# Earlier LayerNorm batches and three-tile steps in the narrow groups of a graph-convolution kernel

## The reference

```python
def _layernorm(x, axis=-1, eps=1e-05):
    m = jnp.mean(x, axis=axis, keepdims=True)
    v = jnp.var(x, axis=axis, keepdims=True)
    return (x - m) / jnp.sqrt(v + eps)

    h = jnp.maximum(_layernorm(x, axis=-1), 0.0)
    support = jnp.matmul(h, W)
    out = jax.nn.relu(jnp.matmul(adj, support) + b)
    return x + out
```

## Time and profile before

| | before |
|---|---|
| median of 3 runs | 775.92 us (775.54 to 781.69) |
| the profiled execution | 775.09 us, of which span 773.3 us |
| mean granted TensorE clock | 0.979 |
| PE busy | 733.7 us (95%), 3120 products |
| DVE busy | 619.8 us (80%) |
| ACT busy | 526.0 us (68%) |
| POOL busy | 129.4 us (17%) |
| moved | 281.59 MB, 364 GB/s over the span |

### The profile page before, as it was taken

The page is one execution under the profiler, slowest core; times in us unless marked ns, Lnnn a source line. Parts: engine busy times, 40 slices in busy tenths (PEclk is TensorE's granted clock), DMA queues, the critical chain, the costliest instruction groups (busy, mean ns, idle before and its releaser), DMA issues.

```text
span 773.3 us, 7777 instructions
## 1 busy us (share of the span) xinstructions
PE 733.7 (95%) x3120; PEld 595.4 (77%) x3120; DVE 619.8 (80%) x297; ACT 526.0 (68%) x375; POOL 129.4 (17%) x86
## 2 busy tenths in 40 slices
PE   4899999999999999999999999999999999999997
PEld 3677777777777777888887888888888888888884
DVE  4778787878787877889877998888888888788885
ACT  5767676767676766676667777666666767677664
POOL 2444444444444444000000000000000000000000
PEclk9899999999999999999999999999999999999999
DMA  8999898999988887899999999999999999899993
GB/s 324 426 339 359 347 354 338 353 341 343 345 345 345 342 333 313 328 390 410 383 379 418 422 410 413 382 391 378 394 382 380 394 388 376 327 374 403 407 340 149
DMA packets 35604, 281.59 MB, mean 364 GB/s; under 512 B 4080, under 2 KB 4464, under 8 KB 11248
## 3 DMA queue, kind: packets, MB, share of 16 engines
q1 hardware_dynamic: 35568, 281.10, 92.9%
HBM read 276.89 MB, written 4.19 MB: 364 GB/s over the span
## 4 chain that ended last, share of the span: by engine, by line
PE 51%; issue 19%; POOL 16%; DMA 7%; DVE 3%; ACT 2%; SPq 1%; POOLq 0%; ACTq 0%; DVEq 0%
PE banks L444 50%; POOL z_sb L235 11%; DMA raw<-adj 7%; POOL rstd L227 5%; DVE low L416 3%; ACT high L308 2%; PE banks L462 0%; POOLq L72 0%; PE banks L464 0%; PE banks L463 0%; SPq L160 0%; SPq L179 0%; DVE sum_low L377 0%; ACT relu_out L279 0%; DVE x_sb L384 0%
## 5 line engine op out<-in xcount | busy, mean ns | idle before, releaser
L416 DVE TENSOR_TENSOR low<-raw,high 128x3072 fp32r<-128x3072 f32 (+1 forms) x190 | 570.1, 3004 | 110.0 <-PE banks L444 68.5
L308 ACT ACTIVATE high<-raw 128x3072 fp32r<-128x3072 f32 (+1 forms) x190 | 471.1, 2488 | 143.8 <-DMA raw<-adj 118.4
L444 PE MATMUL banks<-high,h_high 128*128 128x512 f32 x1024 | 272.0, 397 | 33.9 <-ACT h_high L256 22.8
L444 PE MATMUL banks<-high,h_low 128*128 128x512 f32 x1024 | 276.1, 402 | 0.0
L444 PE MATMUL banks<-low,h_high 128*128 128x512 f32 x1024 | 266.8, 393 | 1.2 <-DVE low L416 1.1
L444 PEld LDWEIGHTS banks<-high,h_high 128*128 128x128 f32 x1024 | 192.6, 189 | 82.2 <-issue 28.7
L444 PEld LDWEIGHTS banks<-high,h_low 128*128 128x128 f32 x1024 | 199.6, 195 | 42.9
L444 PEld LDWEIGHTS banks<-low,h_high 128*128 128x128 f32 x1024 | 194.6, 191 | 45.1 <-DVE low L416 3.9
L235 POOL TENSOR_SCALAR z_sb<-x_sb,neg_mean,rstd 128x128 f32<-128x128 f32 x64 | 90.6, 1426 | 1.8
L256 ACT ACTIVATE h_high<-z_sb 128x512 fp32r<-128x512 f32 (+2 forms) x17 | 10.3, 604 | 90.7 <-POOL z_sb L235 90.6
L227 POOL TENSOR_TENSOR rstd<-var_eps,minus_half 128x4 f32<-128x4 f32 (+2 forms) x17 | 38.4, 2260 | 166.5 <-DVE var_eps L353 166.5
(11 more groups left out here) (17 smaller groups left out, 28.7 us busy)
## 6 DMA issues: line engine op xcount, KB each, us to landing
raw<-adj SPq DMA_DIRECT2D x127, 1536.0 KB, 8.4
raw<-adj SPq DMA_DIRECT2D x63, 1024.0 KB, 6.5
x_sb<-x_blocks SPq DMA_DIRECT2D x16, 256.0 KB, 6.4
out_blocks<-x_sb SPq DMA_DIRECT2D x16, 256.0 KB, 7.6
x_sb<-x_rows SPq DMA_DIRECT2D x15, 256.0 KB, 9.0
raw<-adj SPq DMA_DIRECT2D x4, 512.0 KB, 6.9
raw<-adj SPq DMA_DIRECT2D x2, 256.0 KB, 3.4
x_sb<-x_rows SPq DMA_DIRECT2D x1, 192.0 KB, 3.3
```

What stands on the lines that cost most here:

```text
L308: nc.scalar.activation(high[:, t % HIGH_SLOTS, 0:columns(t)], raw[:, t % RAW_SLOTS, 0:columns(t)], ACT.Copy).then_inc(high_ready, 1)
L416: nc.vector.tensor_tensor(low[:, t % LOW_SLOTS, 0:columns(t)], raw[:, t % RAW_SLOTS, 0:columns(t)], high[:, t % HIGH_SLOTS, 0:columns(t)]. ...
L444: return nc.tensor.matmul(banks[:, FIRST_BANK[g] + c, :], h[:, (t - FIRST_STEP[g]) * DEPTHS[g] + k, :], tile[:, slot, at:at + BANK], start ...
```

## The change

Two things are changed together.

1. The LayerNorm batches are begun earlier. With j = t//4 + 3, mean of batch j is at t%4 = 0, the squares at t%4 = 1 and 2, the variance at t%4 = 2, and rectify and rectified_low of the batch before, j-1, at that same t%4 = 2. Batch m+3 has its mean at step 4m, its variance at 4m+2, its h at 4m+6, and PE takes it from step 4m+8 on. The loads of x are issued one batch earlier, the squares and the variance of batch 2 are moved ahead of step 1, and so are the mean of batch 3 and, on SP, the x of batches 3 and 4.
2. The narrow groups take three k-tiles a step: 21 steps of 3072 columns and a last one of one k-tile (depth_of), 22 in place of 32. The 2 x 22 narrow steps come at 3072 columns, as the wide ones do. Drains are at the steps 3, 6, 8, 11, 13, 16 of a group (in wide groups too), relu at +4, the store at +9. The host lays adj out accordingly.

```diff
@@ -13,10 +13,10 @@
 
 
 WIDTHS = [6, 2, 6, 2]
-DEPTHS = [1, 2, 1, 2]
+DEPTHS = [1, 3, 1, 3]
 FIRST_BLOCK = [0, 6, 8, 14]
 FIRST_BANK = [0, 6, 0, 6]
-STEPS = [TILES // d for d in DEPTHS]
+STEPS = [-(-TILES // d) for d in DEPTHS]
 FIRST_STEP = [sum(STEPS[:g]) for g in range(len(WIDTHS))]
 ALL_STEPS = sum(STEPS)
 LAST = ALL_STEPS - 1
@@ -33,8 +33,8 @@
 Z_SLOTS = 2
 
 
-DRAIN_AT, DRAIN_EVERY = 3, 4
-PROJECT_AFTER, RELU_AFTER, STORE_AFTER = 1, 5, 10
+DRAIN_AT = [3, 6, 8, 11, 13, 16]
+PROJECT_AFTER, RELU_AFTER, STORE_AFTER = 1, 4, 9
 OUT_SLOTS = 2
 EPS = 1e-5
 
@@ -49,6 +49,12 @@
     return max(g for g in range(len(WIDTHS)) if FIRST_STEP[g] <= t)
 
 
+def depth_of(t):
+
+    g = group_of(t)
+    return min(DEPTHS[g], TILES - (t - FIRST_STEP[g]) * DEPTHS[g])
+
+
 def x_slot(j):
 
     return max(j - 1, 0) % X_SLOTS
@@ -58,7 +64,7 @@
 
     for g in range(len(WIDTHS) - 1):
         for c in range(WIDTHS[g]):
-            if FIRST_STEP[g + 1] + DRAIN_AT + c * DRAIN_EVERY + after == t:
+            if FIRST_STEP[g + 1] + DRAIN_AT[c] + after == t:
                 return FIRST_BLOCK[g] + c
     return None
 
...
@@ -182,13 +185,15 @@
                     load_x(1)
                 if i == 1:
                     load_x(2)
+                if i == 2:
+                    load_x(3)
             sp.dma_start(W_sb[:, :], W).then_inc(params_landed, 16)
             sp.dma_start(bias[:, :], b).then_inc(params_landed, 16)
             for t in range(1, ALL_STEPS):
                 g = group_of(t)
                 s = t - FIRST_STEP[g]
-                if g == 0 and s % 4 == 1 and s // 4 + 3 < len(BATCHES):
-                    load_x(s // 4 + 3)
+                if g == 0 and s % 4 == 1 and s // 4 + 4 < len(BATCHES):
+                    load_x(s // 4 + 4)
                 if t >= RAW_SLOTS:
 
                     sp.wait_ge(low_ready, t - RAW_SLOTS + 1)
@@ -289,6 +294,7 @@
             opening(3)
             act.wait_ge(params_landed, 32)
             nc.scalar.activation(W_high[:, :], W_sb[:, :], ACT.Copy).then_inc(W_high_ready, 1)
+            square(2, range(4, 8))
             for t in range(1, ALL_STEPS):
                 g = group_of(t)
                 s = t - FIRST_STEP[g]
@@ -308,15 +314,16 @@
                     nc.scalar.activation(high[:, t % HIGH_SLOTS, 0:columns(t)],
                                          raw[:, t % RAW_SLOTS, 0:columns(t)],
                                          ACT.Copy).then_inc(high_ready, 1)
-                j = (t - 1) // 4 + 2
-                if g == 0 and j < len(BATCHES):
-                    first = BATCHES[j][0]
-                    if t % 4 == 1:
-                        square(j, range(first, first + 2))
+                if g == 0:
+
+                    j = t // 4 + 3
+                    if t % 4 == 1 and j < len(BATCHES):
+                        square(j, range(BATCHES[j][0], BATCHES[j][0] + 2))
                     if t % 4 == 2:
-                        square(j, range(first + 2, first + 4))
-                    if t % 4 == 0:
-                        rectify(j)
+                        if j < len(BATCHES):
+                            square(j, range(BATCHES[j][0] + 2, BATCHES[j][1]))
+                        if j - 1 < len(BATCHES):
+                            rectify(j - 1)
                 n = drained_at(t, 0)
                 if n is not None:
                     act.wait_ge(products_done, FIRST_STEP[group_of(t)])
@@ -391,10 +398,12 @@
             mean(1)
             opening(1)
             variance(1)
+            mean(2)
             opening(2)
             rectified_low(1)
             opening(3)
-            mean(2)
+            variance(2)
+            mean(3)
             dve.wait_ge(W_high_ready, 1)
             nc.vector.tensor_tensor(W_low[:, :], W_sb[:, :], W_high[:, :].bitcast(F32),
                                     ALU.subtract).then_inc(W_low_ready, 1)
@@ -417,14 +426,15 @@
                                             raw[:, t % RAW_SLOTS, 0:columns(t)],
                                             high[:, t % HIGH_SLOTS, 0:columns(t)].bitcast(F32),
                                             ALU.subtract).then_inc(low_ready, 1)
-                j = (t - 1) // 4 + 2
-                if g == 0 and j < len(BATCHES):
+                if g == 0:
+                    j = t // 4 + 3
+                    if t % 4 == 0 and j < len(BATCHES):
+                        mean(j)
                     if t % 4 == 2:
-                        variance(j)
-                    if t % 4 == 0:
-                        rectified_low(j)
-                        if j + 1 < len(BATCHES):
-                            mean(j + 1)
+                        if j < len(BATCHES):
+                            variance(j)
+                        if j - 1 < len(BATCHES):
+                            rectified_low(j - 1)
                 n = drained_at(t, 0)
                 if n is not None:
                     sum_to_low(n)
...
-        rows = adj[first * BANK:(first + width) * BANK].reshape(width, BANK, STEPS[g], depth, P)
-        arrays[f"adj{g}"] = np.ascontiguousarray(rows.transpose(2, 4, 0, 3, 1)) \
-            .reshape(STEPS[g], P, width * depth * BANK)
+        rows = adj[first * BANK:(first + width) * BANK].reshape(width, BANK, TILES, P)
+        for part, k0, k1, deep in (("", 0, TILES // depth * depth, depth), ("_end", TILES // depth * depth, TILES, 1)):
+            if k1 > k0:
+                tiles = rows[:, :, k0:k1].reshape(width, BANK, (k1 - k0) // deep, deep, P)
+                arrays[f"adj{g}{part}"] = np.ascontiguousarray(tiles.transpose(2, 4, 0, 3, 1)) \
+                    .reshape((k1 - k0) // deep, P, width * deep * BANK)
     ap = {name: nc.dram_tensor(name, a.shape, F32, kind="ExternalInput").ap() for name, a in arrays.items()}
     out = nc.dram_tensor("out_blocks", (COL_BLOCKS, P, BANK), F32, kind="ExternalOutput").ap()
-    gnn_layer(nc, ap["x_rows"], ap["x_blocks"], [ap[f"adj{g}"] for g in range(len(WIDTHS))],
-              ap["W"], ap["b"], out)
+    adj_groups = [[ap[f"adj{g}{part}"][s] for part in ("", "_end") if f"adj{g}{part}" in arrays
+                   for s in range(arrays[f"adj{g}{part}"].shape[0])] for g in range(len(WIDTHS))]
+    gnn_layer(nc, ap["x_rows"], ap["x_blocks"], adj_groups, ap["W"], ap["b"], out)
     result = run_bass_kernel_spmd(nc, [arrays], core_ids=[0]).results[0]["out_blocks"]
     return np.ascontiguousarray(result.transpose(0, 2, 1)).reshape(N, P)
```

## The result

| | before | after |
|---|---|---|
| median | 777.03 us (775.54 to 781.69, 4 runs) | 730.97 us (730.1 to 731.72, 4 runs) |
| the profiled execution | 775.09, span 773.3 | 730.47, span 728.7 |
| mean granted TensorE clock | 0.979 | 0.999 |
| PE / DVE / ACT / POOL busy | 95 / 80 / 68 / 17% | 98 / 85 / 72 / 18% |

The ratio of after to before is 0.9397, 95% interval 0.9354 to 0.9441: 6.0% faster. 731 was predicted, with 728 to 741 as the range.

A forecast was written before the change was run, and what follows sets the result against it. Group 0 was taken as bound by a chain over POOL, asked too late, and group 2 by PE. 773.3 - 37.7 - 3.0 - 3.6 = 729.0 us of span, plus 1.8, gave 731, range 728 to 741.

The forecast's parts named there:

- Group 0 from batch 2: 60 wide steps on PE without waits take 244.8 us in place of 282.56: -37.7 us.
- the clock: Lower TensorE clock in group 0 after PE stands still: 14.9 us lost, counted within the group 0 gain.
- one fall at the start: PE falls once to the lower clock level at the start, costing 1.7 to 3 us; allowed for in the range.
- POOL's cover: Group 0, variance to h: POOL takes 12 us, PE runs out only at about 17; cover 8 us a batch.
- rival 4: POOL in group 0 may wait out two DVE instructions: 20.9 us a batch, 30 us more, 798; chance 0.02.
- rival 2: Each POOL instruction in group 0 makes DVE's low wait its length: 21 us more, 752; chance 0.04.
- Transfers of group 0: A batch moves 6.55 MB, 15.3 us at 427 GB/s, under PE's 16.3, so PE is the limit.
- Rival 1: Transfers bound group 0 at 387 GB/s: 16.9 us a batch, 9 us more, 740; chance 0.10.
- The start: Before batch 2: PE starts step 1 at 18.5, batch 2 begins at 31.4 in place of 34.41: -3.0 us.
- Narrow groups: Three k-tiles a step remove small losses, 1.4 in group 1, 0.9 behind it, 1.3 at the end: -3.6 us.
- Drains: SP waits for a store in four places; costed at nothing, 2 us a place or 8 us without cover.
- Sum: Whole kernel: 773.3 - 37.7 - 3.0 - 3.6 = 729.0 us of span, 730.8 with 1.8 outside it; 731 predicted.

The follow-up runs named there:

- Both single experiments: Against the kernel before: only the earlier LayerNorm batches, 736.71 us, ratio 0.9505; only the deeper narrow steps with the new drain steps, 769.38 us, ratio 0.9929.

## Why the prediction was right, point by point

**Group 0 from batch 2: right.** 244.8 us were predicted for 60 steps, 244.80 measured. The sum was made from PE's side, old stretch less new, and it does not depend on how the old loss is split. The split was wrong: the prediction put 14.9 us down to the clock as a part of its own. The run with extra products shows that full speed brings at most 6.7 of it in group 0, since POOL's chain sets the period and the clock's loss lay mostly inside the wait. The 1.7 to 3 us that the range allowed for one fall at the start was given without a row. In the traces of four runs (only the deeper steps, h at its use, one and three more loads) many products of step 1 start 0.43 us apart, as at the lower clock: the step takes 5.8 to 6.3 us in place of 4.9, so 0.9 to 1.4.

**POOL's cover: right in its sign, too large in its limit.** I expected 12 us from variance to z; it is 8.8 in most batches and 11.9 in one. The doubled z give the other side: at 16.7 us PE has already lost 2.0, so the cover ends near 14.7 by my estimate, where I had put 17. That is some 6 us a batch above 8.8, and not 8. ACT comes to h_high 12 to 13.5 us after the variance, where I had put some 10.

**Port rivals.** POOL held by DVE is real, and it can wait out two low at once (6.81), which is the mechanism of rival 4. In the changed kernel it cost PE nothing: its four z take 7.27 us together in most batches. The opposite order, a POOL instruction that holds DVE (rival 2), exists too, against the prediction's reading of its one case; it is only short. The longest case stands in the run with only the earlier batches, one z and the low that begins 0.12 us behind it:

```profile
81.46 0.45 POOL L240 TENSOR_SCALAR z_sb<-x_sb,neg_mean,rstd 128x128 f32<-128x128 f32 x1
81.58 3.54 DVE L425 TENSOR_TENSOR low<-raw,high 128x3072 fp32r<-128x3072 f32 x1
```

This low ends 3.65 us after the z began. Of all runs' low, the 32 that start 0.12 to 0.26 us into a z that was not held up end 3.65 to 3.68 us after its beginning, whatever the distance, as if each had waited until some 0.3 us into the z. Those that start 0.33 us into it or later take their 3.36, but for one of 3.39. The low at 120.97, on which the prediction rested, stood beside rstd, which works on 128x4 values, and not beside a z. The Trainium skill ("SBUF — State Buffer", Who interferes with whom) has the two exclude each other by who issues first. For z and low the traces agree in both orders (z 6.81 us in place of 0.44, low 3.54 in place of 3.36), with some 0.3 us of z's 0.44 as the part that counts; beside rstd, where the earliest low begins 0.18 us into it, no low shows a delay. What rival 2 had wrong is its price: of the 60 low of group 0 from batch 2 on, the changed kernel has three above 3.37 us (3.40 to 3.47).

**Transfers of group 0: right.** Taken was 427 GB/s as the capacity; it is 420. Rival 1 read a limit of 387 from the share of 0.90 at 348. The share is no scale of that kind: it is 1.00 at 404, 1.01 at 414 to 419, and 0.99 at 391.

**The start: 2.5 us, not 3.0, and no closer than executions repeat.** ACT's first high began at 16.05 and not at 15.7 (one more x load and one moved forward), PE at 18.86 and not 18.5. In the run with only the earlier batches the same instructions give 15.39, 18.21 and batch 2 at 31.26, a gain of 3.15 beside the same trace of before. The term can be told to about 1 us only.

**Narrow groups: 4.4 us, not 3.6.** 1.2 in group 1, 1.3 in group 2 (0.9 expected), 1.9 in the rest (1.3 expected). Both single experiments show the same 4.4 from group 1 on; how it divides between depth and drain steps is open.

**Drains, costed at nothing: right.** SP's own waits in the changed kernel:

```profile
SPq L172 <- DMA out_blocks<-x_sb: 18.5, 4, 5.0
```

These are the four places foreseen, on average 4.6 us each, and no PE wait follows.

**Sum.** 37.8 + 2.5 + 4.4 = 44.6 us of span against 44.3 predicted: three terms near their values, with errors of 0.5 and 0.8 of opposite sign. That the median came within 0.1 us of 731 is luck beside that: the large term was right by its working, the small ones cancel, and the start alone varies by more. The prediction also named 0.8 us between the execution read and the median and did not add it; it is 0.5 after the change.

## What to carry to other kernels

Follow the chain to who was asked too late, not to who is slow: the slowest engine of that chain, at 17% busy, needed no faster code but two more steps of distance between its input and its consumer. When a stall and a lower clock go together, don't add them up as if each were to be had alone; the loop that causes the stall may hide the clock. Hold a small term against how far two executions of the same instructions differ (here 0.7 us and more at the start) before explaining it. Count what a ring of slots must cover (landing, and each engine's turn) before the rate: with one slot fewer the same transfers fell from over 400 to 329 GB/s.

## What the runs showed of the hardware that I had not expected

- A GpSimd instruction that reads SBUF can wait out two VectorE instructions with two SBUF inputs that follow each other without a gap (6.81 us, where it takes 0.44 alone). The longest rstd, a tensor_tensor of GpSimd, took 4.14, the rest of one low and its own time. The other way round a low that begins just behind a z takes up to 3.54 in place of 3.36.
- The median time from issue to landing of a 1.5 MB transfer in group 0 (from 60 us on) is nearly the same with three slots in use at 329 GB/s (8.5 us) as with four at 404 (8.9). Near the limit it is not: with three more loads a batch, at 418 GB/s, it is 11.0.
- The busy share of the transfer engines is no measure of what is left: 0.90 at 348 GB/s, 1.00 at 404, while 420 can be had.
